# A fused vision tower on one core: sums of squares in two fp16 parts, a subtraction moved to VectorE, image corrections spread over slots

## The reference, cut to what matters

```python
h = _L0_tok_ref(x, gamma, beta, W, b)                 # per image: mean, variance, then the patch convolution
h = concatenate([cls_tok, h], axis=1)                 # 64 x 170 x 128
h = h + _L0_attn_ref(_layernorm(h), ...)              # graph convolution, relu, projection
h = h + _L0_ffn_ref(_layernorm(h), ...)

# inside _L0_ffn_ref
q = _l2norm(hx @ Wq) * scale * qn_g                   # x / sqrt(sum(x*x) + 1e-12), for each head of 64
k = _l2norm(hx @ Wk) * scale * kn_g
attn = softmax(causal(q @ k.T * dh ** -0.5))
y = (attn @ v) @ Wo
gate = softmax(y @ gate_W + gate_b)
hid = gelu(y @ W1[e] + b1[e])                         # 8 experts of 512 hidden features
out = sum over e of gate[e] * (hid @ W2[e] + b2[e])
```

## Time and profile before

| | before |
|---|---|
| median of 3 runs | 1449.69 us |
| profiled execution: time / span | 1456.65 us / 1454.9 us |
| TensorE matmul busy | 1419.2 us, 98% |
| VectorE busy | 1223.4 us, 84% |
| ScalarE busy | 1105.7 us, 76% |
| GpSimd busy | 284.9 us, 20% |
| TensorE's granted clock, mean | 0.991 |

### The profile page before, as it was taken

The page is one execution under the profiler, slowest core; times in us unless marked ns, Lnnn a source line. Parts: engine busy times, 40 slices in busy tenths (PEclk is TensorE's granted clock), DMA queues, the critical chain, the costliest instruction groups (busy, mean ns, idle before and its releaser), DMA issues.

```text
span 1454.9 us, 31173 instructions
## 1 busy us (share of the span) xinstructions
PE 1419.2 (98%) x10945; PEld 986.4 (68%) x10945; DVE 1223.4 (84%) x2592; ACT 1105.7 (76%) x1880; POOL 284.9 (20%) x285
## 2 busy tenths in 40 slices
PE   7999999999999999999999999999999999999998
PEld 5665667676676677676676677676676677676665
DVE  7887798888888888988888888988888888987777
ACT  5344678787878888787878888787878888787766
POOL 1124042130301212131301212131301212130100
PEclk9999899999999999999999999999999999999989
DMA  8796142433333242433333242433333242433320
GB/s 252 175 245 137 51 110 35 116 48 106 48 106 48 53 98 31 115 48 106 48 106 48 58 96 29 117 47 106 48 106 48 63 90 29 118 46 99 52 84 11
DMA packets 39763, 122.76 MB, mean 84 GB/s; under 512 B 5680, under 2 KB 6192, under 8 KB 37552
## 3 DMA queue, kind: packets, MB, share of 16 engines
q0 software_dynamic: 21312, 53.03, 24.1%
q1 hardware_dynamic: 18272, 69.28, 13.2%
q10 hardware_dynamic: 144, 0.01, 0.0%
HBM read 68.98 MB, written 47.70 MB: 80 GB/s over the span
## 4 chain that ended last, share of the span: by engine, by line
PE 75%; DVE 12%; issue 6%; DMA 5%; ACT 2%; DVEq 0%; SPq 0%; ACTq 0%; POOLq 0%
PE pair L1105 25%; PE pair L1070 22%; PE pair L838 9%; PE pair L825 4%; DVE area L1548 3%; PE pair L1016 3%; DMA area<-gate_scratch 2%; PE pair L1004 2%; PE pair L933 2%; PE pair L989 2%; DVE area L1561 1%; DMA area<-area 1%; PE pair L964 1%; ACT area L681 1%; DMA gate_scratch<-gt_t 1%
## 5 line engine op out<-in xcount | busy, mean ns | idle before, releaser
L676 ACT ACTIVATE area<-pair,pack_b_sb 128x680 f32<-128x680 f32 x512 | 423.3, 827 | 182.1 <-PE pair L1070 182.0
L1548 DVE TENSOR_TENSOR area<-area 128x680 f16<-128x680 f32 x512 | 454.1, 892 | 104.9 <-ACT area L681 99.1
L1070 PE MATMUL pair<-area,ws 128*128 128x340 f16 x3072 | 531.8, 308 | 5.1 <-ACT area L676 2.6
L1105 PE MATMUL pair<-area,ws 128*128 128x340 f16 x3072 | 526.4, 307 | 7.4 <-DVE area L1561 4.7
L1105 PEld LDWEIGHTS pair<-area,ws 128*128 128x128 f16 x3072 | 289.6, 97 | 161.2 <-DVE area L1561 28.0
L1070 PEld LDWEIGHTS pair<-area,ws 128*128 128x128 f16 x3072 | 292.9, 97 | 155.1 <-ACT area L676 7.8
L681 ACT ACTIVATE area<-pair,pack_b_sb 128x680 f16<-128x680 f32 x384 | 315.7, 822 | 0.0
L507 POOL DMA_DIRECT2D tower_out<-area x120 | 106.8, 890 | 925.3 <-DVE area L1561 909.5
L1561 DVE SCALAR_TENSOR_TENSOR area<-pair,pack_b_sb,area 128x340 f32<-128x340 f32 x256 | 133.9, 565 | 9.8 <-PE pair L1105 8.6
L642 ACT ACTIVATE area<-pair,nbias,root 85x85 f32<-85x85 f32 (+1 forms) x256 | 112.3, 467 | 0.2
L464 POOL TENSOR_TENSOR area<-area 128x680 f16<-128x680 f32 x56 | 89.1, 1598 | 45.3 <-ACT area L605 43.0
(11 more groups left out here) (239 smaller groups left out, 1757.5 us busy)
## 6 DMA issues: line engine op xcount, KB each, us to landing
tower_out<-area POOLq DMA_DIRECT2D x120, 340.0 KB, 4.5
area<-gate_scratch SPq DMA_DIRECT2D x16, 1360.0 KB, 9.9
area<-gate_scratch SPq DMA_DIRECT2D x16, 1020.0 KB, 7.2
area<-cells SPq DMA_DIRECT2D x16, 392.0 KB, 7.2
area<-cells POOLq DMA_DIRECT2D x14, 392.0 KB, 6.7
area<-area POOLq DMA_DIRECT2D x14, 392.0 KB, 6.4
area<-gate_scratch SPq DMA_DIRECT2D x16, 340.0 KB, 4.5
tower_out<-ht SPq DMA_DIRECT2D x15, 340.0 KB, 2.3
```

Source lines behind the costliest of these rows:

```text
L676: nc.scalar.activation(two(hid[slot % NHID]), halves(hid_ps[slot % 2]), ACT.Gelu_apprx_tanh, bias=col(COL_B1 + slot)).then_inc(hid_ready, 1)
L1070: last = mm(hid_ps[slot % 2][:, j, 0:TH], lhs[:, w], rhs[:, j * TH:(j + 1) * TH], start=(i == 0), stop=(i == 2))
L1105: last = mm(eo_ps[:, j, 0:TH], lhs[:, w], rhs[:, j * TH:(j + 1) * TH], start=(m % CH == 0 and i == 0), stop=(m % CH == CH - 1 and i == 2))
L1548: v.tensor_tensor(hl[slot % NPART], hid[slot % NHID], hh[slot % NPART], ALU.subtract).then_inc(hlo_ready, 1)
```

## The change

The queries' and the keys' squares are now made twice by ScalarE, in fp16 (high part) and in fp32. VectorE subtracts the two (`q_lo` in slot 7, `k_lo` in slot 9), and TensorE sums both parts with fp16 matmuls against `head_16`. This holds for groups 1 to 15; group 0, in the prologue, keeps the fp32 sums. The tokens' low part moves from GpSimd, where it stood behind the second expert's store, to VectorE's slot 15. The corrections are taken apart into `fixa` and `fixb` and lie in slots 6 to 12 instead of 6 to 9. `tok_hi` moves from slot 11 to 13, `root1` from 11 to 13, `root2` from 12 to 14, `wide` from 14 to 15, `kn` from 15 to 16 and the queries' and keys' `cast` from 16 to 17.

```diff
-QK_SLOTS = {"q": 7, "sums_q": 9, "k": 9, "sums_k": 11, "root0": 11, "root1": 11, "root2": 12, "wide": 14,
-            "cast": 16, "kn": 15}
-EARLY_SLOTS = {"fix0": 6, "fix1": 7, "fix2": 8, "fix3": 9, "tok_hi": 11, "mean": 18, "dev": 17, "sq": 19,
+QK_SLOTS = {"q": 7, "q_lo": 7, "sums_q": 9, "k": 9, "k_lo": 9, "sums_k": 11, "root0": 11, "root1": 13, "root2": 14,
+            "wide": 15, "cast": 17, "kn": 16}
+EARLY_SLOTS = {"fixa0": 6, "fixb0": 8, "fixa1": 8, "fixb1": 10, "fixa2": 10, "fixb2": 11, "fixa3": 11,
+               "fixb3": 12, "tok_hi": 13, "tok_lo": 15, "mean": 18, "dev": 17, "sq": 19,
...
+        head_16 = sb("head_16", [128, H], F16)
+        sqk_h, sqk_l = (h1[:, 2 * T:3 * T].bitcast(F16)[:, k * T:(k + 1) * T] for k in range(2))
+        sqq_h, sqq_l = (h1[:, 3 * T:4 * T].bitcast(F16)[:, k * T:(k + 1) * T] for k in range(2))
...
 GpSimd, prologue
-            pool.wait_ge(pool_prep, 16)
+            pool.tensor_copy(head_16[:, :], head_m[:, 0:DH + 1:DH]).then_inc(pool_prep, 1)
+            pool.wait_ge(pool_prep, 17)
 GpSimd, weigh
-                    if e == 1 and ahead:
-                        tokens_lo(g + 2)
 ScalarE, queries_keys (the same for k)
                     act.wait_ge(q_ps, g + 1)
+                    if later:
+                        nc.scalar.activation(two(sqq_h), halves(fr_ps), ACT.Square, bias=att_b[:, 0:1])
                     nc.scalar.activation(two(sqq), halves(fr_ps), ACT.Square, bias=att_b[:, 0:1]).then_inc(ss_ready, 1)
 TensorE, queries_keys
+                def sums_parts(n, hi, lo):
+                    for t in range(TILES):
+                        c, tile = SUMS_AT + 2 * (n * TILES + t), slice(t * QC, (t + 1) * QC)
+                        mm(fr_ps[0:QC, 0, c:c + 2], hi[:, tile], head_16[:, :], start=True, stop=False)
+                        last = mm(fr_ps[0:QC, 0, c:c + 2], lo[:, tile], head_16[:, :], start=False, stop=True)
+                    return last
...
+                if step == "sums_q" and later:
+                    pe.wait_ge(q_ready, g + 1)
+                    pe.wait_ge(sl_ready, 2 * g - 1)
+                    sums_parts(0, sqq_h, sqq_l)
...
+                if step == "sums_k" and later:
+                    pe.wait_ge(k_ready, g + 1)
+                    pe.wait_ge(sl_ready, 2 * g)
+                    sums_parts(1, sqk_h, sqk_l).then_inc(ss_ps, 1)
 VectorE, early
-                    v.scalar_tensor_tensor(fix_b, conv_u[:, :], img[...], conv_b[:, :], ALU.mult, ALU.add).then_inc(fix_step, 1)
-                    dve.wait_ge(fix_step, NB * g + (b + 1))
-                    v.scalar_tensor_tensor(h_b, h_b, img[...], fix_b, ALU.mult, ALU.add).then_inc(fixed, 1)
+                    if step[3] != "b":
+                        v.scalar_tensor_tensor(fix_b, conv_u[:, :], img[...], conv_b[:, :], ALU.mult, ALU.add).then_inc(fix_step, 1)
+                    if step[3] != "a":
+                        dve.wait_ge(fix_step, NB * g + (b + 1))
+                        v.scalar_tensor_tensor(h_b, h_b, img[...], fix_b, ALU.mult, ALU.add).then_inc(fixed, 1)
+                if step == "tok_lo":
+                    dve.wait_ge(tokh_ready, g - 1)
+                    v.tensor_tensor(two(part_l), tokens(g), two(part_h), ALU.subtract).then_inc(tokl_ready, 1)
 VectorE, queries_keys
+                if step == "q_lo":
+                    dve.wait_ge(ss_ready, 2 * g + 1)
+                    v.tensor_tensor(sqq_l, sqq, sqq_h, ALU.subtract).then_inc(sl_ready, 1)
+                if step == "k_lo":
+                    dve.wait_ge(ss_ready, 2 * (g + 1))
+                    v.tensor_tensor(sqk_l, sqk, sqk_h, ALU.subtract).then_inc(sl_ready, 1)
```

More of the change, by code:

```diff
@@ L285, in vit_tower @@
         q_ps, q_ready, k_ps, k_ready = map(sem, ("q_ps", "q_ready", "k_ps", "k_ready"))
-        ss_ready, ss_ps, wide_ready, kn_ready = map(sem, ("ss_ready", "ss_ps", "wide_ready", "kn_ready"))
+        ss_ready, sl_ready, ss_ps, wide_ready, kn_ready = map(sem, ("ss_ready", "sl_ready", "ss_ps", "wide_ready", "kn_ready"))
         vp_ps, vp_ready, score_ps, max_ready = map(sem, ("vp_ps", "vp_ready", "score_ps", "max_ready"))
@@ L449, in _ @@
             pool.tensor_copy(ident16[:, :], ident[:, :]).then_inc(pool_prep, 1)
-            pool.wait_ge(pool_prep, 16)
+            pool.tensor_copy(head_16[:, :], head_m[:, 0:DH + 1:DH]).then_inc(pool_prep, 1)
+            pool.wait_ge(pool_prep, 17)
             pool.tensor_copy(identb[:, :], ident[0:QC, 0:QC]).then_inc(consts_ready, 1)
-            def tokens_lo(g):
-                pool.wait_ge(tokh_ready, g - 1)
-                pool.tensor_tensor(two(part_l), tokens(g), two(part_h), ALU.subtract).then_inc(tokl_ready, 1)
             def relu_parts(g, c):
@@ L615, in graph, with queries_keys @@
                     var_evac(g, "ln2", var2_ps, TILES, 1.0 + EPS_LN, 2)
-            def queries_keys(g, step):
+            def queries_keys(g, step, later=True):
                 if step == "q":
                     act.wait_ge(q_ps, g + 1)
+                    if later:
+                        nc.scalar.activation(two(sqq_h), halves(fr_ps), ACT.Square, bias=att_b[:, 0:1])
                     nc.scalar.activation(two(sqq), halves(fr_ps), ACT.Square, bias=att_b[:, 0:1]).then_inc(ss_ready, 1)
@@ L624, in queries_keys @@
                     act.wait_ge(k_ps, g + 1)
+                    if later:
+                        nc.scalar.activation(two(sqk_h), halves(fr_ps), ACT.Square, bias=att_b[:, 1:2])
                     nc.scalar.activation(two(sqk), halves(fr_ps), ACT.Square, bias=att_b[:, 1:2]).then_inc(ss_ready, 1)
@@ L704, in chain @@
                 for step in steps_in(QK_0, n):
-                    queries_keys(0, step)
+                    queries_keys(0, step, later=False)
                 for step in steps_in(FIRST_1, n):
@@ L939, in queries_keys @@
                     of_hx(0).then_inc(q_ps, 1)
-                if step == "sums_q":
+                if step == "sums_q" and not later:
                     pe.wait_ge(ss_ready, 2 * g + 1)
@@ L943, in queries_keys @@
                     sums(0, sqq)
+                if step == "sums_q" and later:
+                    pe.wait_ge(q_ready, g + 1)
+                    pe.wait_ge(sl_ready, 2 * g - 1)
+                    sums_parts(0, sqq_h, sqq_l)
                 if step == "k":
                     of_hx(D).then_inc(k_ps, 1)
-                if step == "sums_k":
+                if step == "sums_k" and not later:
                     pe.wait_ge(k_ready, g + 1)
@@ L1377, in early @@
                 if step[:3] == "fix":
-                    b = int(step[3])
+                    b = int(step[-1])
                     fix_b, h_b = fix[:, b * NP * NP:(b + 1) * NP * NP], ht[:, bass.ds(g * T + (b * TOK + 1), NP * NP)]
-                    v.scalar_tensor_tensor(fix_b, conv_u[:, :], img[:, bass.ds(g * NB + (B + b), 1)], conv_b[:, :],
-                                           ALU.mult, ALU.add).then_inc(fix_step, 1)
-                    dve.wait_ge(fix_step, NB * g + (b + 1))
-                    v.scalar_tensor_tensor(h_b, h_b, img[:, bass.ds(g * NB + b, 1)], fix_b,
-                                           ALU.mult, ALU.add).then_inc(fixed, 1)
+                    if step[3] != "b":
+                        v.scalar_tensor_tensor(fix_b, conv_u[:, :], img[:, bass.ds(g * NB + (B + b), 1)], conv_b[:, :],
+                                               ALU.mult, ALU.add).then_inc(fix_step, 1)
+                    if step[3] != "a":
+                        dve.wait_ge(fix_step, NB * g + (b + 1))
+                        v.scalar_tensor_tensor(h_b, h_b, img[:, bass.ds(g * NB + b, 1)], fix_b,
+                                               ALU.mult, ALU.add).then_inc(fixed, 1)
+                if step == "tok_lo":
+                    dve.wait_ge(tokh_ready, g - 1)
+                    v.tensor_tensor(two(part_l), tokens(g), two(part_h), ALU.subtract).then_inc(tokl_ready, 1)
                 if step == "dev":
```

## The result

The changed kernel takes 1455.66 us (median of 20 runs), the one before 1450.87 in the runs beside it: a ratio of 1.0031, with a 95% interval of 1.0025 to 1.0038. It is slower, by about 4.5 us; the ratio leaves out one of the 20 runs, which took 1476.32 us at a granted clock of 0.945. Periods are therefore what I compare.

What follows compares the result with a forecast made beforehand. TensorE, busy for 98% of the span, was taken to set the period by its own order. The terms 13 x 0.34 + 0.4 - 0.3 = +4.5 us took 1449.69 to 1454.2 us, with an 8 in 10 range of 1441 to 1458.

Steps and rivals of the forecast that it cites:

- TensorE's saving: Two sums a period, each down from 1.17 to 0.65 us as fp16 matmuls: 1.04 us a period.
- rival E: The fp16 sums are no cheaper and the stalls stay: +19 us, 1469; chance 0.02.
- Hidden costs: ScalarE's extra squares, 0.73 us each, hidden in idle time; VectorE's work grows by 0.2 us a period.
- Step 1: At `sums_q`, TensorE waits for VectorE's `q_lo`: a stall of 0.14 us, and 0.05 behind it.
- Step 2: At `sums_k`, `k_lo` ends in time: no stall, balance -0.85 us.
- Step 3: At slot 14's weigh, late behind `root1`: TensorE stalls 0.26 us, and 0.05 behind it.
- Step 4: At `mean`, which waits for `kn`, late behind `root2`, `wide` and slot 16's gelus: stall 0.83 us, and 0.05 behind.
- The middle period: Stalls outweigh the faster sums in a regular period of 81.73 us: +0.34 us.
- The first period: GpSimd also splits weights here and VectorE is behind already: +0.4 us.
- The last period and what follows it: No early steps, thus no `mean` and no stall at `sums_q`; slot 18's weigh late: -0.3 us.
- Rival B: `kn` is in time and the saving stays: 0.54 or 0.85 us a period gained, 1442 to 1438; chance 0.22.
- Rival D: More stalls, at slot 18's write of the buffer slot 16's gelus read: 1458 to 1466; chance 0.08.

Runs made afterwards that it cites:

- e1: The changed kernel with its fp32 sums put back, the extra squares and subtractions still made but unused: 1471.31 us.
- e3: The changed kernel without the subtractions `q_lo` and `k_lo`, TensorE summing the high parts twice: 1452.50 us.
- e2: The changed kernel with `kn` in slot 15 instead of 16 and `tok_lo` in slot 14 instead of 15: 1450.40 us.
- e6: The changed kernel with GpSimd's four first-period weight splits behind stores 0, 1, 3, 4 instead of 0, 1, 2, 3: 1457.26 us, one run.
- e5: The changed kernel with casts of slots 11 and 14 moved to 15 and 16, `root1` to slot 12, `tok_hi` and `tok_lo` to 14: 1438.76 us.
- e9: The fp16 sums alone, under the slots of the kernel before and with `tok_lo` on GpSimd: 1466.75 us.
- e7: The changed kernel with the subtraction for the tokens' low part given back to GpSimd, behind the second store: 1475.32 us.

## Why the prediction was right

It forecast 1454.2 us, slower by 4.5; measured was a ratio of 1.0031, 4.5 us. Step by step:

- **TensorE's saving**: 1.04 us a period forecast. The two sums took 1.17 and 1.16 and take 0.68 and 0.65 (the first behind a wait): 1.00. e1 gives 1.08. The matmuls go at 0.041 us each, as in the earlier trace rows. By the rule of the Trainium skill, TensorE: Matmul & The Clock Gate, LDWEIGHTS, a load of 85 columns would take an estimated 0.071 us. The trace doesn't agree with it here, and rival E didn't occur.
- **Hidden costs**: ScalarE's two squares and VectorE's two subtractions of squares. e3 shows the second pair to cost 0.15 us, all of it in step 1. VectorE's busy time grew by 0.8 us a period (70.05 to 70.84) where I had 0.2, mostly because it never contained the waits that I took off. The squares' cover was argued from the timeline and not taken away in an experiment.
- **Step 1**: 0.14 forecast, 0.14 measured.
- **Step 2**: no stall forecast, none measured (679.56 - 678.70 = 0.86 ahead of `sums_k`).
- **Step 3**: 0.26 forecast, 0.27 measured.
- **Step 4**: 0.83 forecast, 0.77 measured; and the group behind `mean` takes 0.58, without the 0.05 that I added for it. `wide` and the gelus behind it are 0.05 and 0.01 to 0.02 us shorter from start to start in a busy queue (690.69 - 689.73 = 0.96) than in the rows that I took them from. e2 shows that this wait is a matter of order.
- **The middle period**: +0.34 forecast, +0.21 measured. The mechanism was right and this size off by 0.13 us, 1.7 us over 13 periods.
- **The first period**: +0.4 forecast, +1.93 or +1.61 measured, depending on which profile of the kernel before it is set against. This is the term that I sized worst. I had seen that GpSimd blocks VectorE there, and had the stall at slot 15's output right (1.74, against 1.71 in the earlier trace rows), but had not followed which instruction GpSimd's split would meet: `root2`, the link in front of ScalarE's wait of 2.77 us. e6 takes the split away from `root2`, and the stall at the turn goes with it.
- **The last period and what follows it**: -0.3 forecast. From the last period's first store to the end of the span it is 127.24 us after, 127.97 and 127.73 in the two profiles of before: -0.5 to -0.7.

In sum, from the first store to the end of the span, it is 1277.86 us after, and 1273.86 and 1273.85 in the two profiles of before: +4.0, where I had 13 x 0.34 + 0.4 - 0.3 = +4.5. The measured ratio allows 3.6 to 5.5. What comes ahead of the first store can't be compared so closely: 174.74 and 181.05 us in two executions of one kernel. That the total came out as near as this is partly luck, for two errors cancel: the middle periods were forecast 1.7 us too long, the first one 1.2 to 1.5 too short.

Rival B, `kn` in time, did not occur, but it was the right place to look: e5 is that case, reached by another order, and gains what B said, 0.8 us a period against before. Rival D did not occur as written: in the middle period above, slot 18's input matmuls start at 692.39, 0.87 us after the group before them, without a stall. Its kind of lateness, ahead of the gelus of slot 16, came up in the first period only, and TensorE met it at the turn.

## What to carry to other kernels

Where one engine sets the time and the others follow written queues, cost a moved instruction by following the chain of results it stands in, link by link, to the engine that sets the time; busy shares say little (84 and 85% on VectorE here, with a stall that neither more time nor less work for it would move). Ask of every late result whether something stands ahead of it in its queue that it doesn't need. And look at the odd period too: the first one cost 1.6 to 1.9 us here, as much as eight or nine of the regular ones at 0.21.

## What the runs showed that I had not expected

A blocked VectorE instruction lost nearly all the time that GpSimd's had left, and short ones lost as much as long ones. A subtraction of 0.87 us took 2.29, so it lost 1.42, where GpSimd's had 1.56 left (e9). One of 0.19 took 1.47 and lost 1.28 of 1.43 (e7). Two of 0.18 and 0.19 took 0.59 and 1.03 beside the weight splits and lost 0.41 of 0.54 and 0.84 of 0.99. It isn't only instructions with two inputs: the first root step in the earlier trace rows, with one, took 1.49 beside GpSimd's, and 0.17 in the changed kernel. GpSimd's can lose as well: in e9 its subtraction started within a cast of VectorE (686.57 to 687.08) and took 1.93 instead of 1.47.

Giving one GpSimd instruction of 1.47 us back cost 1.3 us a period (e7). That is more than the whole saving that the change was built on.
